# The third stage of a four-stage network on one Trainium2 core: routing first, experts behind 6.5 base tiles, and no arithmetic on GpSimd

## The chip, the core and the metric

The kernel runs on one core of a Trainium2 chip. The metric is the device time of one execution in microseconds (us), the median of several runs. The engines are TensorE (PE, matrix products), VectorE (DVE), ScalarE (ACT), GpSimd (POOL) and SyncE (SP, which here only issues DMAs); each has its own queue of instructions, and they wait for each other on semaphores.

## The reference

Four layers work one after the other on x of 2048 tokens by 1024 numbers (16 tiles of 128 tokens). Each is a mixing over 64 channels and then a feed-forward part, and is added to x. The change is in the third layer and in what it hands to the fourth:

```python
# third layer, feed-forward part (x: tokens y2, made by a convolution)
base_out = jnp.einsum('bsi,oi->bso', x, base_w) + base_b
res_hidden = jnp.einsum('bsi,ri->bsr', x, A)                 # 64 numbers a token
logits = jnp.einsum('bsi,ei->bse', x, router_w)              # 16 experts
topw, topi = jax.lax.top_k(jax.nn.softmax(logits, axis=-1), 2)
topw = topw / (jnp.sum(topw, axis=-1, keepdims=True) + 1e-06)
combine = jnp.sum(jax.nn.one_hot(topi, num_experts) * topw[..., None], axis=-2)
delta = jnp.einsum('bse,bsr,eor->bso', combine, res_hidden, B)
return base_out + delta * SCALING
# fourth layer: a 64x64 mixing matrix for each of the 32 sequences, then
return _layernorm(shared_out + routed_out, ln_gamma, ln_beta)
```

## The kernel before

Float32 products are made of two float32r parts, a high one that ScalarE rounds and a low one that VectorE subtracts; a product of two such pairs is three matmuls (hi·hi, hi·lo, lo·hi).

The third stage (`phase_l2`) has these parts. **Router**: `router` makes 80 columns a tile (16 logits, 64 numbers of `res`). `choose`, `weigh`, `rank` and `place_pairs` on VectorE, with `rank_pairs` on TensorE between them, find the two experts of every token and the place `pos` of its 4096 (token, expert) pairs in a list ordered by expert. GpSimd scatters the pairs there (32 indirect DMAs of 128 rows, to `scratch_pairs`). **Base**: for each of the 16 tiles `base_chunk(t, 0)` and `(t, 1)`, 24 matmuls of 128x512 each, into PSUM `po[t % 2]`; their input is y2 of the tile, loaded into one buffer (`l_y`), cut into `l_y2s_hi` and `l_y2s_lo`. `base_out` on VectorE adds the product to `x3[t]`, to which GpSimd (`base_bias`) has added the bias. **Experts**: 47 tiles of 128 pairs, in 12 groups of up to four. `turn_rows(g)` transposes the rows of a group (twice, a transpose for PSUM rows 0 to 63 and a product with the identity for rows 64 to 127), `r_high` and `r_low` cut them, `expert_tile(i)` makes four matmuls into one of three pairs of PSUM banks, ACT and DVE (`expert_out`) copy one half each into one of four buffers, and GpSimd writes the 128 rows to `scratch_expert_out` by an indirect DMA, whose row numbers lie in column 64 of the group's rows. `rows_in(g)` reads a group's rows into one of three buffers, once the expert rows of group g-3 are written. **Sum and mix**: per tile two rows of `delta` are read (`deltas_in`), GpSimd adds them (`delta_sum`), VectorE adds the sum to x3 (`add_deltas`), `mix(t)` makes 8 products of 128x128 on TensorE with the fourth layer's matrices, `y3_out` and `y3_low` (DVE) and a cut on ACT prepare the fourth layer's input, and GpSimd adds `beta` to x3, which SP stores for the fourth layer (`scratch_x3b`).

Every engine's order is written out by hand. Before, TensorE does base tiles 0 to 7 (the router of the last tiles and the ranking among them), then all experts, then eight blocks of one base tile and two mixes. The queue of SP holds all loads but those of B (4 DMAs of 2 MB, on ACT).

```python
def y2_in(t):
    sp.wait_ge(y2_lo, 2 * t)
    sp.dma_start(y2[:], tile_of(SC["y2T"], t))...
def rows_in(g):
    if g >= 3:
        sp.wait_ge(tr_mm, g - 2)
        for sem in eo_stored:
            sp.wait_ge(sem, 16 * (g - 2))
```

The fourth stage (`phase_l3`) is a long row of matmuls; at the end of each half of the tokens ACT loads x3b tile by tile and `finish(T)` on DVE adds it to the normalized tile.

## Time and profile before

| | |
|---|---|
| median of 3 runs | 1807.75 us (1804.79 to 1808.0) |
| the profiled execution | 1816.88 us, its span 1815.2 us |
| TensorE busy in the span | 1644.1 us (91%) |
| third stage, from the last convolutions to the gate of the fourth | 480.2 to 899.5 us |
| of it: up to the experts' first transpose | 480.2 to 604.4 us |
| of it: experts | 604.4 to 711.5 us |
| of it: eight blocks of a base tile and two mixes | 711.5 to 899.5 us |
| fourth stage's matmuls | 899.5 to 1797.6 us |

All times in the profile count from the span's start. "Busy" of TensorE includes the modelled end of each matmul: in an unbroken row a matmul of 128x512 is shown with 0.39 us, and the next starts 0.23 us after it.

### The profile page before, as it was taken

What the parts mean: (1) busy time and instruction counts of PE and PEld (TensorE: products, weight loads), DVE (VectorE), ACT (ScalarE), POOL (GpSimd) and SP (SyncE); (2) the same over time, 40 slices, a digit from 0 to 9 for tenths busy, and PEclk for the clock granted to TensorE, in tenths of its full rate; (3) what the DMA queues carried; (4) which work ended last, traced back from release to release, by engine and by line L of the source; (5) the groups of instructions that cost most, each with busy time, mean ns of one, the idle gap of its engine ahead of it and who ended that gap; (6) DMA issues with size and microseconds to landing.
All of it is one profiled execution on the core that took longest, in us unless ns stands there. A gap on an engine that the chain in (4) does not pass through costs nothing.

```text
span 1815.2 us, 20711 instructions
## 1 busy us (share of the span) xinstructions
PE 1644.1 (91%) x7830; PEld 1326.3 (73%) x7830; DVE 839.6 (46%) x1294; ACT 500.3 (28%) x763; POOL 423.2 (23%) x272
## 2 busy tenths in 40 slices
PE   6799678999897978776899999999999999999997
PEld 3688546988875646655678888888767888888875
DVE  5455458995274433654523333333282333333326
ACT  2344223333225332110032222221243222222112
POOL 1000111234245244555611111111251111111110
PEclk9999889999997988878999999999999999999999
DMA  8577444457831355455621111111462111111114
GB/s 280 132 176 168 152 77 151 161 179 234 312 141 53 115 214 197 165 187 202 232 91 47 47 47 46 46 46 47 134 214 70 47 47 47 46 46 46 47 58 162
DMA packets 108210, 222.82 MB, mean 123 GB/s; under 512 B 21892, under 2 KB 60924, under 8 KB 107260
## 3 DMA queue, kind: packets, MB, share of 16 engines
q1 hardware_dynamic: 86612, 161.00, 27.9%
q0 software_dynamic: 13120, 38.88, 6.6%
q10 hardware_dynamic: 8400, 21.89, 3.7%
q8 instruction: 51, 0.84, 0.2%
q14 instruction: 27, 0.22, 0.0%
HBM read 152.96 MB, written 76.61 MB: 126 GB/s over the span
## 4 chain that ended last, share of the span: by engine, by line
PE 67%; DMA 7%; DVE 4%; POOL 3%; issue 2%; ACT 2%; SPq 1%; another core or an unknown queue 1%; ACTq 0%; POOLq 0%; DVEq 0%
PE pd L1775 25%; PE pu L1775 24%; PE pf L1775 6%; PE l_po L1775 4%; DMA delta<-scratch_expert_out 3%; PE pw L390 2%; PE pw L391 2%; POOL l_x L1371 1%; PE l_ea L1213 1%; DMA scratch_expert_out<-expert_out,pair_rows 1%; PE l_po L1714 1%; DMA l_y<-scratch_y2T 1%; DMA pair_rows<-scratch_pairs 1%; PE pg L997 1%
## 5 line engine op out<-in xcount | busy, mean ns | idle before, releaser
L1910 POOL TENSOR_TENSOR down_lo<-raw,down_hi 128x1024 fp32r<-128x1024 f32 x40 | 100.3, 2508 | 698.2 <-ACT down_hi L1923 698.2
L1775 PE MATMUL pd<-down_hi,hid_hi 128*128 128x512 f32 x640 | 249.1, 389 | 2.9 <-issue 2.9
L1775 PE MATMUL pu<-y_hi,up_hi 128*128 128x512 f32 x640 | 249.2, 389 | 0.0
L1775 PE MATMUL pu<-y_hi,up_lo 128*128 128x512 f32 x640 | 249.0, 389 | 0.0
L1775 PE MATMUL pd<-down_hi,hid_lo 128*128 128x512 f32 x640 | 249.0, 389 | 0.0
L1775 PE MATMUL pd<-down_lo,hid_hi 128*128 128x512 f32 x640 | 249.0, 389 | 0.0
L1775 PE MATMUL pu<-y_lo,up_hi 128*128 128x512 f32 x640 | 249.0, 389 | 0.0
L2079 DVE TENSOR_TENSOR hid_lo<-hidden,hid_hi 128x512 fp32r<-128x512 f32 x64 | 44.3, 692 | 393.3 <-ACT hid_hi L1987 393.3
L2018 DVE TENSOR_TENSOR acc<-pd,acc 128x512 f32<-128x512 f32 x224 | 143.6, 686 | 54.7 <-PE pd L1775 51.4
L1981 ACT ACTIVATE hidden<-pu 128x512 f32<-128x512 f32 x64 | 38.3, 598 | 464.9 <-PE pu L1775 464.9
L1775 PEld LDWEIGHTS pd<-down_hi,hid_hi 128*128 128x128 f32 x640 | 120.2, 188 | 28.6 <-issue 3.7
L1775 PE MATMUL l_po<-l_base_hi,l_y2s_hi 128*128 128x512 f32 x256 | 108.3, 423 | 34.8 <-DVE l_y2s_lo L1463 32.9
L1775 PEld LDWEIGHTS pu<-y_hi,up_lo 128*128 128x128 f32 x640 | 120.2, 188 | 25.1
L1775 PEld LDWEIGHTS pu<-y_hi,up_hi 128*128 128x128 f32 x640 | 120.0, 188 | 25.1
L1775 PEld LDWEIGHTS pd<-down_hi,hid_lo 128*128 128x128 f32 x640 | 120.1, 188 | 25.1
L1775 PEld LDWEIGHTS pu<-y_lo,up_hi 128*128 128x128 f32 x640 | 120.2, 188 | 24.9
L1775 PEld LDWEIGHTS pd<-down_lo,hid_hi 128*128 128x128 f32 x640 | 120.1, 188 | 24.7
L1775 PE MATMUL pf<-cbT,z_hi 128*128 128x512 f32 x256 | 104.8, 409 | 5.0 <-DVE z_lo L880 5.0
L1775 PE MATMUL l_po<-l_base_lo,l_y2s_hi 128*128 128x512 f32 x256 | 106.4, 416 | 2.2 <-issue 2.2
L1775 PE MATMUL l_po<-l_base_hi,l_y2s_lo 128*128 128x512 f32 x256 | 105.5, 412 | 1.9 <-issue 1.9
L1775 PE MATMUL pf<-cbT,z_lo 128*128 128x512 f32 x256 | 101.8, 398 | 0.0
L1775 PEld LDWEIGHTS l_po<-l_base_hi,l_y2s_hi 128*128 128x128 f32 x256 | 52.2, 204 | 47.9 <-issue 36.0
(306 smaller groups left out, 2689.4 us busy)
## 6 DMA issues: line engine op xcount, KB each, us to landing
X<-scratch_x SPq DMA_DIRECT2D x256, 64.0 KB, 2.6
l_x<-scratch_x SPq DMA_DIRECT2D x32, 512.0 KB, 5.8
delta<-scratch_expert_out SPq DMA_DIRECT2D x32, 512.0 KB, 7.2
raw<-in_up SPq DMA_DIRECT2D x32, 512.0 KB, 3.7
raw<-in_down SPq DMA_DIRECT2D x32, 512.0 KB, 4.2
x_in<-in_x SPq DMA_DIRECT2D x16, 512.0 KB, 4.7
scratch_x<-x_in SPq DMA_DIRECT2D x16, 512.0 KB, 4.4
scratch_x<-l_x SPq DMA_DIRECT2D x16, 512.0 KB, 5.6
```

The source lines that it names most:

```text
L390: pe.matmul(cols, x[:, b * GROUPS + g, :], taps[0][:, g, :], start=True, stop=False)
L391: last = pe.matmul(cols, xs[:, b * GROUPS + g, :], taps[1][:, g, :], start=False, stop=True)
L997: last = pe.matmul(pg[n % 2][:], chunk[:, l, (k - at) * P:(k - at + 1) * P], K["exp"][:, l, :], start=l == 0, stop=l == NLAT - 1)
L1213: last = pe.matmul(ea[t % 2][:, 0:R2 + E2], prior["y2"][:, t % 2, k, :], war[:, k, :], start=k == 0, stop=k == KC - 1)
L1371: pool.tensor_tensor(x3[t][:], x3[t][:], beta[:], ALU.add).then_inc(x3b_made, 1)
L1714: last = pe.matmul(out_banks[i % 3][h][:], rT[g % 2][part][:, n * P:(n + 1) * P], B[:].rearrange("p e o -> p (e o)")[:, bass.ds(at + h * H ...
L1775: mm = pe.matmul(out, lhs[a], rhs[b], start=first and n == 0, stop=last and n == len(pairs) - 1)
L1910: pool.tensor_tensor(dn[u][i][1][:], raw[i][:], dn[u][i][0][:].bitcast(F32), ALU.subtract).then_inc(dn_lo, 1)
L1981: act.activation(act_f[:, k % 2, :], pu[q], ACT.Relu).then_inc(relu, 1)
L2018: last = dve.tensor_tensor(part, bank, part, ALU.add)
L2079: dve.tensor_tensor(hid[u][1][:, i, cols], pu[q] if lat else act_f[:, k % 2, :], hid[u][0][:, i, cols].bitcast(F32), ALU.subtract).then_in ...
```

## The change

- **Routing**: the last router products come before any further base work, and `choose` directly behind the last convolution's output.
- **Experts** start behind 6.5 base tiles (before: 8). The second half of base tile 6 is spread over the first eight groups, a few matmuls each; `po[0]` stays with it, so experts have two pairs of banks. The blocks behind are nine: the first has base tile 7 alone, the others a base tile and two mixes.
- **Rows**: ScalarE writes each row twice side by side (`pair_rows_twice`), and one transpose of 128 columns turns it. VectorE copies the row numbers out (`row_numbers`), so a buffer of rows is free without waiting for the stores.
- **y2** is loaded in halves, each when the same half of the tile before is cut. B comes in 8 DMAs of 1 MB on SP's queue, between them.
- **Bias** is a product of ones and two rows (high and low), two matmuls more per base tile.
- **GpSimd** computes nothing in this stage: VectorE adds both deltas itself, GpSimd's queue issues the stores of x3 and y3, ACT's queue the loads of the mixing matrices. `beta` is added in the fourth stage, by a DMA that adds to its destination.

```diff
-        def y2_in(t):
+        def y2_in(t, c):
             sp.wait_ge(prior["y2_stored"][t % 2], 16 * (t // 2 + 1))
-            sp.wait_ge(y2_lo, 2 * t)
-            sp.dma_start(y2[:], tile_of(SC["y2T"], t)).then_inc(y_loaded, 16)
+            sp.wait_ge(y2_lo, 2 * (t - 1) + c + 1)
+            sp.dma_start(y2[:, chunk(c)], tile_of(SC["y2T"], t)[:, chunk(c)]).then_inc(y_loaded[c], 16)
...
             if g >= 3:
-                sp.wait_ge(tr_mm, g - 2)
-                for sem in eo_stored:
-                    sp.wait_ge(sem, 16 * (g - 2))
+                sp.wait_ge(twice, g - 2)
+                sp.wait_ge(row_ids, g - 2)
...
-        delta_sum(0)
-        delta_sum(1)
...
+        for s in range(9):
+            for t in mixed_tiles(s):
+                pool.wait_ge(x3_made, t + 1)
+                pool.wait_ge(x3p_made, 2 * (t + 1))
+                pool.dma_start(tile_of(SC["x3b"], t), x3[t][:]).then_inc(x3b_stored[t % 4], 16)
...
         def add_deltas(t):
-            dve.wait_ge(d_sum, t + 1)
-            dve.wait_ge(x3p_made, 2 * (t + 1))
-            dve.tensor_tensor(x3[t][:], x3[t][:], d[t % 2][0][:], ALU.add).then_inc(x3_made, 1)
+            dve.wait_ge(d_loaded[t % 2], 32 * (t // 2 + 1))
...
+            dve.tensor_tensor(x3[t][:], x3[t][:], d[t % 2][0][:], ALU.add).then_inc(d_first, 1)
+            dve.wait_ge(d_first, t + 1)
+            dve.tensor_tensor(x3[t][:], x3[t][:], d[t % 2][1][:], ALU.add).then_inc(x3_made, 1)
...
-                pe.transpose(tr[g % 2][0:R2, cols], G[:, g % 3, n, 0:R2], K["ident"][:])
-                last = pe.matmul(tr[g % 2][R2:P, cols], G[:, g % 3, n, 0:R2], K["ident"][:], start=True, stop=True)
+                last = pe.transpose(tr[g % 2][:, n * P:(n + 1) * P], Gd[:, g % 2, n, :, :].rearrange("p u r -> p (u r)"), K["ident"][:])
...
-        router(pe, NT - 3)
-        base_chunk(0, 1)
         prior["conv"](pe, NT - 1)
         router(pe, NT - 2)
+        router(pe, NT - 1)
+        base_chunk(0, 1)
         base_chunk(1, 0)
-        router(pe, NT - 1)
+        rank_pairs()
         base_chunk(1, 1)
-        base_chunk(2, 0)
-        rank_pairs()
-        base_chunk(2, 1)
-        for t in range(3, 8):
+        for t in range(2, 6):
             base_chunk(t, 0)
             base_chunk(t, 1)
+        base_chunk(6, 0)
         turn_rows(0)
...
+            if g == 0:
+                base_start(6, 1)
+            if g < 8:
+                base_part(6, 4 + g // 2, g % 2)
+            if g == 8:
+                base_bias(6)
+        for s in range(9):
+            base_chunk(7 + s, 0)
+            base_chunk(7 + s, 1)
+            for t in mixed_tiles(s):
+                mix(t)
...
+        def add_beta(T):
+            pool.wait_ge(x3b_loaded[T % 2], 16 * (T // 2 + 1))
+            pool.dma_start(x3b[:, T % 2, :], A["L3_ffn_ln_beta"].partition_broadcast(P), accum_op=ALU.add).then_inc(beta_added[T % 2], 16)
...
-            dve.wait_ge(x3b_loaded[T % 2], 16 * (T // 2 + 1))
+            dve.wait_ge(beta_added[T % 2], 16 * (T // 2 + 1))
```

VectorE's queue around the last convolution (y2T) and the routing. Before:

```order
L705 TENSOR_TENSOR y2T<-pw,ctx 128x8x64 x2
L1463 TENSOR_TENSOR l_y2s_lo<-l_y,l_y2s_hi 128x512
L1469 TENSOR_TENSOR l_x_0<-l_po,l_x_0 128x512 x2
L1463 TENSOR_TENSOR l_y2s_lo<-l_y,l_y2s_hi 128x512
L1486 MEMSET route_taken 128x8
L1487 TENSOR_REDUCE route_m<-router_lg 128x16
```

And now:

```order
L1660 TENSOR_TENSOR l_bias<-l_bias_row,l_bias 1x1024
L1496 TENSOR_TENSOR l_y2s_lo<-l_y,l_y2s_hi 128x512
L706 TENSOR_TENSOR y2T<-pw,ctx 128x8x64 x2
L1519 MEMSET route_taken 128x8
L1520 TENSOR_REDUCE route_m<-router_lg 128x16
```

The two cuts of y2 and the first base tile's addition, which stood between the last convolution and the choice of experts, now stand behind the choice.

SP's queue in the blocks behind the experts, for two blocks. Before:

```order
L1237 DMA l_y<-scratch_y2T 128x1024
L1253 DMA delta<-scratch_expert_out 128x1024 x4
L1261 DMA mats<-scratch_mats 64x64 x2
L1262 DMA l_bias<-scratch_bias 128x128
L1266 DMA scratch_x3b<-l_x_2 128x1024
L1261 DMA mats<-scratch_mats 64x64 x2
L1262 DMA l_bias<-scratch_bias 128x128
L1266 DMA scratch_x3b<-l_x_3 128x1024
L1232 DMA l_x_11<-scratch_x 128x1024
L1232 DMA l_x_12<-scratch_x 128x1024
```

And now:

```order
L1258 DMA l_y<-scratch_y2T 128x512
L1275 DMA delta<-scratch_expert_out 128x1024 x4
L1258 DMA l_y<-scratch_y2T 128x512
L1246 DMA l_x_9<-scratch_x 128x1024
L1246 DMA l_x_10<-scratch_x 128x1024
L1258 DMA l_y<-scratch_y2T 128x512
L1275 DMA delta<-scratch_expert_out 128x1024 x4
```

The stores of x3 and the loads of the mixing matrices are no longer in this queue between two loads of deltas.

GpSimd's queue in the same place. Before:

```order
L1335 TENSOR_TENSOR delta<-delta 128x1024 x2
L1331 TENSOR_TENSOR l_x_9<-l_x_9,l_bias 128x1024
L1371 TENSOR_TENSOR l_x_2<-l_x_2,l_beta 128x1024
L1371 TENSOR_TENSOR l_x_3<-l_x_3,l_beta 128x1024
L1335 TENSOR_TENSOR delta<-delta 128x1024 x2
L1331 TENSOR_TENSOR l_x_10<-l_x_10,l_bias 128x1024
```

And now:

```order
L1383 DMA scratch_x3b<-l_x_8 128x1024
L1383 DMA scratch_x3b<-l_x_9 128x1024
L1387 DMA scratch_y<-l_y_0 128x1024
L1387 DMA scratch_y<-l_y_1 128x1024
L1383 DMA scratch_x3b<-l_x_10 128x1024
```

All additions have gone and two stores per block (four from tile 8 on) have come.

## Rows read from the trace of the kernel before

**Rows 1.** Stages: window, us, busy (count) PE PEld DVE ACT POOL, clock, DMA, GB/s

```profile
480.20:604.40 124.20, 103.78 (x458) 83.84 (x457) 62.76 (x104) 47.24 (x73) 53.22 (x43) 0.86 0.38 141
604.40:711.50 107.10, 89.13 (x347) 56.86 (x346) 42.08 (x63) 34.74 (x60) 45.93 (x47) 0.89 0.50 178
711.50:899.50 188.00, 136.33 (x625) 115.44 (x624) 96.85 (x85) 16.38 (x22) 105.12 (x39) 0.85 0.54 194
```

**Rows 2.** The chain that ended last: start us, us, what

```profile
487.49 4.73 issue
...
563.12 15.56 another core or an unknown queue
...
616.63 3.33 DMA scratch_expert_out<-expert_out,pair_rows
620.05 3.16 DMA pair_rows<-scratch_pairs
...
746.40 9.39 DMA delta<-scratch_expert_out
```

**Rows 3.** TensorE's timeline: start us, us, operation, count [idle before]

```profile
505.18 1.91 PE L1213 MATMUL l_ea<-l_war,y2T 128*128 128x80 f32 x16
...
521.71 0.41 PE L1687 MATMUL l_tr<-route_taken,ranks_below 128*128 128x272 bf16 x1 [3.68 <-DVE route_taken L1511]
...
604.44 0.27 PE L1700 MATMUL l_tr<-ident,pair_rows 128*64 128x128 f32 x1
604.64 0.43 PE L1701 MATMUL l_tr<-ident,pair_rows 128*64 128x128 f32 x2
...
742.32 2.05 PE L1725 MATMUL l_ea<-mats,l_x 128*128 128x128 f32 x16
```

**Rows 4.** Window of the base product alone, three tiles in a row

```profile
523.78:558.30 34.52, 34.49 (x144) 28.12 (x144) 2.56 (x4) 0.00 (x0) 0.95 0.20 61
```

**Rows 5.** GpSimd's timeline in the routing

```profile
513.70 4.92 POOL L1331 TENSOR_TENSOR l_x<-l_x,l_bias 128x1024 f32<-128x1024 f32 x2 [2.25 <-DMA l_x<-scratch_x]
```

**Rows 6.** VectorE's timeline in the routing

```profile
511.94 0.40 DVE L1487 TENSOR_REDUCE route_m<-router_lg 128x16 f32<-128x256 f32 x1
...
513.96 2.41 DVE L1496 TENSOR_TENSOR route_pick<-route_key,route_kmax 128x256 f32<-128x256 f32 x1
...
520.77 0.43 DVE L1509 TENSOR_TENSOR route_pick<-route_key,route_kmax 128x256 f32<-128x256 f32 x1
```

**Rows 7.** GpSimd's timeline: last pairs, first and last expert stores

```profile
532.54 1.07 POOL L1351 DMA_INDIRECT scratch_pairs<-pair_val,pair_pos  x1 [13.92 <-DVE pair_pos L1563]
...
574.67 0.96 POOL L1351 DMA_INDIRECT scratch_pairs<-pair_val,pair_pos  x1 [0.30 <-issue]
612.76 1.00 POOL L1357 DMA_INDIRECT scratch_expert_out<-expert_out,pair_rows  x1 [37.13 <-DVE expert_out L1585]
...
708.56 0.98 POOL L1357 DMA_INDIRECT scratch_expert_out<-expert_out,pair_rows  x1 [0.30 <-issue]
709.84 0.98 POOL L1357 DMA_INDIRECT scratch_expert_out<-expert_out,pair_rows  x1 [0.30 <-issue]
```

**Rows 8.** Waits behind the experts: us, times, longest

```profile
POOL delta L1335 <- DMA delta<-scratch_expert_out: 80.9, 11, 15.2
...
PE l_po L1775 <- DVE l_y2s_lo L1463: 25.8, 6, 6.1
```

**Rows 9.** The tile delta: ns min/median/max, and its DMA

```profile
L1590 DVE TENSOR_TENSOR l_x<-l_x,delta x16: 1211/3230/3420, 720.5 to 892.0; 128x1024 f32<-128x1024 f32 x16
...
DMA to landing us min/median/max: 3.4/7.2/9.4
```

**Rows 10.** The tile x3b of the fourth stage, from issue to landing

```profile
DMA to landing us min/median/max: 3.2/4.1/12.6
```

**Rows 11.** ACT at the end of the kernel

```profile
1800.73 0.33 ACTq L1926 DMA_DIRECT2D l_x3b<-scratch_x3b  x1
```

**Rows 12.** VectorE at the end of the kernel

```profile
1806.90 1.28 DVE L2038 SCALAR_TENSOR_TENSOR acc<-scratch,l_rstd,l_x3b 128x1024 f32<-128x1024 f32 x1
```

More of the change, by code:

```diff
@@ L1288, in sync @@
         sp.wait_ge(r_mm, NT)
+        sp.wait_ge(val_stored, 16 * 2 * NT)
+        for g in range(3):
+            rows_in(g)
+        sp.wait_ge(B_rest, E2)
         x3_in(6)
[L1290 to L1297 removed]
+        y2_in(7, 0)
+        for g in range(3, NGRP):
+            rows_in(g)
+            if g == 6:
+                y2_in(7, 1)
+        y2_in(8, 0)
+        sp.wait_ge(tr_mm, NGRP)
+        x3_in(7)
+        sp.wait_ge(twice, NGRP)
+        sp.wait_ge(row_ids, NGRP)
         x3_in(8)
@@ L1301, in sync @@
         deltas_in(1)
[L1302 to L1313 removed]
+        y2_in(8, 1)
@@ L1897, in body @@
             if end:
+                add_beta(HT * (half - 1))
+                add_beta(HT * (half - 1) + 1)
                 for t in range(HT):
```

492 lines of the change are left out of this document (267 added, 225 removed).

## The prediction

> **What bounds the kernel now.** I read the page's busy times first: TensorE is busy 91% of the span, so what can go is its idle time and its slow stretches. The windows by stage [rows 1] say where these are. The fourth stage has none to speak of (table above: one row of matmuls from 899.5 to 1797.6). The third stage takes 124.2 + 107.1 + 188.0 = 419.3 us, and in each of its parts the granted clock is 0.85 to 0.89, since the engine stops and starts. Then I read the chain that ended last [rows 2] for what stands between the matmuls. In the first part a wait of 4.73 us and one of 15.56 us stand out; TensorE also waits 3.68 us for the choice of experts [rows 3]. Among the experts a loop repeats every two groups: stores of expert rows (3.33 us), then the load of the next rows (3.16 us), then TensorE. Behind the experts the loop is: a load of deltas (9.39 us) that GpSimd waits for, and GpSimd's additions behind it. The waits of that part [rows 8] say the same: GpSimd waits 80.9 us for deltas and TensorE 25.8 us for the cut y2.
>
> **The change, part by part.** I use three measures. Base product: three tiles took 34.52 us [rows 4], 11.5 us each; without that window's small losses it is 48 matmuls by 0.227 us (the spacing in an unbroken row) = 10.9 us. Expert store: 709.84 - 708.56 = 1.28 us each on GpSimd [rows 7]. Mix: the 16 records of one tile take 2.05 us [rows 3], 1.95 without the start; two are 3.9 us.
>
> *First part (480.2 to 604.4).* Removed: 1.5 base tiles moved behind, 17.3 us; the wait of 4.73 us, because ScalarE no longer waits for y2 and 8 MB of B ahead of the last shifted tile; the wait of 3.68 us, because the choice starts right behind the last convolution and base products lie over it. It also gets shorter: VectorE's 128x256 operation takes 2.41 us while GpSimd adds and 0.43 us when it doesn't [rows 5, 6]. Removed, if it is what it looks like, the gap of 15.56 us. It lies inside the 43 us of GpSimd's 32 scatters, and no row names its cause; in the new order the scatters lie over base tiles too. I take it as gone, and price the other case as a rival. Added: two bias matmuls for 6 tiles, 12 by 0.23 = 2.7 us. Sum: 124.2 - 17.3 - 4.7 - 3.7 - 15.6 + 2.7 = 85.6 us, so the first transpose starts at 565.8. The scatter must be through by then. The last router product ended at 505.18 + 1.91 = 507.1 [rows 3]; without the wait of 4.7 us and with two base halves (10.9 us) behind it, it ends near 491.5. From the start of the choice to the first scatter it took 532.54 - 511.94 = 20.6 us [rows 6, 7], of which 4 us were the two stretched operations; so the scatter starts near 508.4. It takes 575.63 - 532.54 = 43.1 us [rows 7] and ends near 551.5; with 3.3 us for its stores and 3.16 us for the load [rows 2] the rows are there near 558. That is 8 us of cover.
>
> *Experts.* Since rows no longer wait for stores, GpSimd's 1.28 us a store should set the pace: 46 by 1.28 = 59 us between first and last. TensorE needs less for a group of four: 16 matmuls by 0.23 (3.7 us), four transposes by 0.20 (0.8 us, the spacing of L1700 and L1701 [rows 3]; before, three records a tile, 2.4 us), and 3 base matmuls (0.7 us), together 5.2 us against 5.13 us of GpSimd. Two PSUM pairs instead of three leave each pair about 1 us to be copied, which is near VectorE's time for it; so there is no slack here. First store 8.3 us after the first transpose before (612.76 - 604.44), less 2.7 us for the shorter transposes: 5.6 us. Last store 3.3 us to land. Sum 5.6 + 59 + 3.3 = 67.9 us, where it was 713.2 - 604.4 = 108.8 us.
>
> *Behind the experts.* TensorE leaves the experts 5.8 us before the last store has landed (four buffers and one copy ahead). Then a block of base tile 7, and eight blocks with a base tile and two mixes. A base tile with bias is 10.9 + 0.46 = 11.4 us; a block with mixes 11.4 + 3.9 = 15.3 us. The deltas must keep up: after the second pair of deltas is added, the next 2 MB are asked for, and the four loads take 7.2 to 9.4 us [rows 9]; VectorE's four additions take 1.21 us each where GpSimd is silent and 3.23 us in the median where it isn't [rows 9], so 4.9 us. With 0.7 us for the cut that SP waits for, this loop is 9.4 + 4.9 + 0.7 = 15.0 us, just under TensorE's 15.3. VectorE as a whole is busy 96.85/8 = 12.1 us a block now [rows 1], and 16 additions more are paid by shorter ones. I take 16 us a block, a little above both. Sum: 2 by 11.4 - 5.8 + 3.9 + 7 by 16 = 132.9 us to the gate, where it was 899.5 - 713.2 = 186.3 us.
>
> *Halves of y2.* The half of the next tile is asked for one whole tile ahead, and the 25.8 us of waits [rows 8] are in the 53 us that this part gives; nothing is counted twice. *B on SP's queue*: 1 MB ahead of a half of y2 is two loads of 512 KB, of which the second of a pair landed in 7.2 us in the median [rows 9], against a cover of 11.4 - 1.5 us for the cut; nothing, though the slowest (9.4 us) would come close. *Stores on GpSimd's queue and matrices on ACT's*: both engines are idle most of this part (16.38 us of 188 busy on ACT [rows 1]); nothing.
>
> *Beta in the fourth stage.* The trace has no adding DMA. The nearest row is the load of the same tile, 3.2 to 12.6 us, 4.1 in the median [rows 10]; below nothing it can't be. In a tile's rhythm of 5.4 us, a load and an addition have two rhythms, 9.6 us, so 4.1 + 4.1 is hidden. At the very end it isn't: the last load is issued at 1800.73 [rows 11] and used at 1806.90 [rows 12], 6.2 us for 3.2 + 0.5 + 4.1 = 7.8 us. I take 2 us there and 2 us at the end of the first half: +4 us (0 to 18). By the Trainium skill (DMA: Bandwidth & Descriptors, anatomy of the GpSimd path) such a DMA costs 2.0 us plus its bytes at 436 GB/s, an estimate of 3.2 us; by that the end would cost 1 us less. No run here shows it yet.
>
> *Total.* First part 124.2 - 85.6 = 38.6, experts 40.9, behind 53.4, less 4: 128.9 us. From the profiled execution's 1816.9 us that is 1688 us. The median of the runs is 9.1 us lower (1807.75), which would give 1679. But if the gap of 15.6 us is only in profiled executions, the runs give 1807.75 - 113.3 = 1694. I take the middle: **1686 us**, own range 1665 to 1702.
>
> **The rivals.**
> - *Deltas hold the blocks.* 4.5 MB a block in 15.3 us is 294 GB/s, where the part ran at 194 [rows 1]; if loads queue longer (14 us for four), a block takes 20 us: 8 by 4 = +32, **1718 us**. For it: every row of delta's chain is at its limit. Against: the DMA share was 0.54.
> - *The gap stays.* Whatever stops the engines inside the scatter does so again: +16, **1702 us**. For it: it lies in the scatter. Against: the scatter starts 30 us before it [rows 2, 7], and TensorE ran through most of these [rows 4].
> - *Experts slower than GpSimd's pace.* Two PSUM pairs, and more work on ACT and DVE: 1.6 us a tile, +15, **1701 us**.
> - *GpSimd's stores are held by VectorE.* Each store waits out an addition, x3's next tile comes late, and a block takes 18 us: +16, **1702 us**. Against it: GpSimd's indirect DMAs took 0.96 to 1.07 us all along [rows 7], while VectorE worked beside them. [...]
> - *Slower than before.* The adding DMA, with 128 rows read from the same 4 KB, could take so long that it sets the rhythm of the fourth stage's 16 last tiles. To eat 129 us, each must lose 8 us: (4.1 + y)/2 = 13.5, so y = 23 us. Above that the kernel is slower than before; at 30 us, 1686 + 16 by 3.5 + 129, about **1870 us**. The worst load of the tile took 12.6 us, which speaks against it.
> - *It does nothing*, because one queue (SP) still couples all loops: its largest waits were for stores of experts, which are gone. **1808 us**.
>
> **How the numbers follow.** Forecast 0.50; deltas 0.20; gap 0.10; experts 0.10; stores held 0.05; slower 0.03; nothing 0.02. The range must hold the first five, of which the slowest reaches some way beyond 1718, and below the forecast the case that all pieces reach TensorE's pace (1686 less 6 for the blocks, 6 for the first part and 9 for the median's lead over the profile): 1665 to 1735. What a measurement of this kernel can tell from no change is 0.2%, 3.6 us. Faster 0.95, same 0.02, slower 0.03.
>
> **What would show it.** Right: no idle time of TensorE over 3 us between 486 and the experts; expert stores 1.28 us apart without the pauses of 5.5 us; starts of base tiles 15.3 to 16 us apart behind them; granted clock near 1 in all three; VectorE's additions at 1.2 us. Wrong: base tiles 20 us apart with TensorE waiting for x3 (deltas); a pause of 15 us inside the scatter; stores 1.6 us apart and TensorE waiting for copies; x3 loads late behind stores; VectorE waiting for beta in each of the 16 last tiles. If TensorE waits for rows at its first transpose, the 8 us of cover were wrong.

## The result, and the profile after

The changed kernel takes **1733.9 us** in the median of 4 runs (1733.3 to 1743.1), the kernel before on the same chip 1807.9 (1804.8 to 1810.2): ratio 0.960, 95% interval 0.956 to 0.963. It is faster, by 74 us; the forecast was 1686 us and a range of 1665 to 1735 us, and 122 us of gain. The profiled execution of the changed kernel took 1743.05 us, 55 us more than the 1688 us that the sum gave for it. (On two other chips the kernel before took 1822 to 1842 us and the changed one 1732 to 1748 us, ratios 0.950 and 0.949.)

The windows of the changed kernel by stage; the columns are those of [rows 1]. The first window ends where the base product of the third stage begins, then come the part up to the first turned rows, the experts, the part behind them, and the fourth stage with the end.

```profile
core 0: us, PE busy (x) PEld busy (x) DVE busy (x) ACT busy (x) POOL busy (x), PEclk, DMA share, GB/s
0.00:483.70 483.70, 418.82 (x2397) 339.18 (x2397) 296.82 (x516) 162.13 (x258) 79.42 (x71) 0.93 0.60 166
483.70:573.60 89.90, 89.90 (x455) 73.39 (x455) 54.11 (x88) 46.23 (x59) 39.21 (x36) 1.00 0.65 210
573.60:658.00 84.40, 66.27 (x263) 44.31 (x262) 42.50 (x73) 39.97 (x71) 44.32 (x46) 0.96 0.66 237
658.00:792.25 134.25, 134.25 (x706) 111.35 (x705) 88.17 (x106) 19.48 (x26) 14.19 (x25) 1.00 0.78 284
792.25:1741.30 949.05, 900.83 (x3955) 732.22 (x3953) 348.45 (x526) 238.85 (x348) 150.23 (x90) 0.98 0.25 77
```

In the first part and behind the experts TensorE now has no idle time at all and a granted clock of 1.00; of the stages that the prediction priced, only the experts and the fourth have any idle time. Set beside the forecast, piece by piece:

| piece, us | before | forecast | measured |
|---|---|---|---|
| start to base product | 471.0 | 471.0 | 483.7 |
| to the first turned rows | 133.5 | 94.9 | 89.9 |
| experts, until TensorE leaves them | 102.5 | 62.1 | 84.3 |
| behind them, to the gate | 192.6 | 138.7 | 134.3 |
| fourth stage to the end | 915.7 | 919.7 | 949.1 |

(Forecast: the prediction's sums with its own borders moved; 62.1 is 67.9 - 5.8.) The miss of 55 us is 12.7 ahead of the base product, in stages that the change hardly touches, 22.2 at the experts and 29.4 in the fourth stage, less 5.0 and 4.4 us where it went better than forecast.

The fourth stage does its upward and downward products in two halves, each closed by a part of eight tiles that are normalized ("first end", before the second gate; "second end", before the end of the kernel). Windows of the changed kernel:

```profile
792.25:1197.56 405.31, 403.86 (x1788) 329.16 (x1786) 135.86 (x201) 103.25 (x146) 53.02 (x25) 1.00 0.17 56
1197.56:1263.56 66.00, 46.99 (x192) 37.67 (x192) 41.79 (x61) 18.63 (x29) 32.78 (x28) 0.88 0.93 252
1263.56:1670.89 407.33, 405.88 (x1784) 329.54 (x1785) 136.79 (x201) 104.67 (x149) 53.03 (x22) 0.99 0.15 51
1670.89:1741.30 70.41, 44.09 (x192) 35.85 (x192) 34.01 (x64) 12.30 (x24) 11.40 (x16) 0.84 0.68 178
```

Both long stretches are as before. The two ends take 66.0 and 70.4 us; from the same starting points (first downward product, at 1304.79 and 1759.15) they took 47.6 and 56.0 before. That is where the 33 us are. What happens to one buffer there is read from three timelines of the changed kernel, in this order ScalarE's queue (load of x3), GpSimd (adding DMA) and VectorE (the use):

```profile
1222.34 0.33 ACTq L2003 DMA_DIRECT2D l_x3b<-scratch_x3b  x1
1235.72 0.33 ACTq L2003 DMA_DIRECT2D l_x3b<-scratch_x3b  x1
```

```profile
1205.27 0.93 POOL L1966 DMA_DIRECT2D l_x3b<-in_L_ffn_ln_beta  x1 [2.47 <-DMA l_x3b<-scratch_x3b]
1226.50 0.86 POOL L1966 DMA_DIRECT2D l_x3b<-in_L_ffn_ln_beta  x1 [3.32 <-DMA l_x3b<-scratch_x3b]
```

```profile
1221.02 1.28 DVE L2115 SCALAR_TENSOR_TENSOR acc<-scratch,l_rstd,l_x3b 128x1024 f32<-128x1024 f32 x1 [10.44 <-DMA l_x3b<-in_L_ffn_ln_beta]
1233.58 2.11 DVE L2115 SCALAR_TENSOR_TENSOR acc<-scratch,l_rstd,l_x3b 128x1024 f32<-128x1024 f32 x1 [1.06 <-DMA l_x3b<-in_L_ffn_ln_beta]
```

The load is asked for at 1222.34 and has landed by 1226.50, when beta is asked for; that has landed by 1233.58, VectorE uses the buffer for 2.1 us, and its next load goes out at 1235.72: 13.4 us for one round, with two buffers and a rhythm of 5.44 us a tile. In the mean of the six rounds of each end a round took 13.3 and 13.7 us: the load 4.1 and 4.7, GpSimd's issue 0.3 behind its landing, the adding DMA 6.8 and 7.1, and VectorE's wait and use 2.1 and 1.5. The very first addition of beta, asked for at 1205.27, had landed by 1221.02, behind 4 MB of y in the same queue. The list of DMA issues has the medians from issue to landing (last column):

```profile
l_x3b<-scratch_x3b ACTq DMA_DIRECT2D x16, 512.0 KB, 4.1
l_x3b<-in_L_ffn_ln_beta POOLq DMA_DIRECT2D x16, 512.0 KB, 6.8
```

At the first end TensorE then waits for VectorE to take its products out of PSUM into `acc`, 19.0 of 19.5 us in all, 12.0 of them ahead of the second gate:

```profile
PE pd L1845 <- DVE acc L2091: 19.5, 4, 12.0
```

```profile
1245.82 0.50 PE L1845 MATMUL pd<-down_hi,hid_hi 128*128 128x512 f32 x1 [1.51 <-DVE acc L2091]
1263.56 0.59 PE L1845 MATMUL pd<-y_hi,gate_hi 128*8 128x512 f32 x1 [12.01 <-DVE acc L2091]
```

At the second end it is not TensorE that waits. Its 192 products take 44.6 us (43.8 before), and the time is lost behind them: 25.8 us to the end of the kernel, where it was 12.2. The last of VectorE's waits for beta lie there:

```profile
1670.89:1715.49 44.60, 44.09 (x192) 35.85 (x192) 25.79 (x52) 10.37 (x20) 8.62 (x12) 1.00 0.74 190
1715.49:1741.30 25.81, 0.01 (x1) 0.00 (x0) 8.21 (x12) 1.93 (x5) 2.78 (x5) 0.56 0.58 158
```

```profile
1718.24 1.28 DVE L2115 SCALAR_TENSOR_TENSOR acc<-scratch,l_rstd,l_x3b 128x1024 f32<-128x1024 f32 x1 [3.86 <-DMA l_x3b<-in_L_ffn_ln_beta]
1724.49 1.28 DVE L2115 SCALAR_TENSOR_TENSOR acc<-scratch,l_rstd,l_x3b 128x1024 f32<-128x1024 f32 x1 [3.51 <-DMA l_x3b<-in_L_ffn_ln_beta]
```

At the experts, the waits of TensorE in the changed kernel between 573 and 660 us (us in all, times, longest), and four of GpSimd's stores:

```profile
PE l_ea L1778 <- DVE expert_out L1623: 6.3, 5, 1.6
PE l_ea L1778 <- ACT expert_out L1423: 4.4, 4, 2.5
PE l_po L1778 <- issue: 3.1, 7, 1.0
```

```profile
600.55 0.98 POOL L1377 DMA_INDIRECT scratch_expert_out<-expert_out,pair_ids  x1 [0.30 <-issue]
602.63 0.97 POOL L1377 DMA_INDIRECT scratch_expert_out<-expert_out,pair_ids  x1 [1.10 <-ACT expert_out L1423]
603.91 0.98 POOL L1377 DMA_INDIRECT scratch_expert_out<-expert_out,pair_ids  x1 [0.30 <-issue]
606.39 0.97 POOL L1377 DMA_INDIRECT scratch_expert_out<-expert_out,pair_ids  x1 [1.50 <-DVE pair_ids L1612]
```

Of the pauses of 6.5 to 9.7 us before, one of 5.25 us near the end is left, but stores now come in twos, 1.3 to 1.7 and then 1.5 to 3.0 us apart: 47 stores from 579.36 to 659.52, 1.74 us each, where the forecast had 1.28.

### The profile page after: what moved, and what is told of

Read it like the earlier page. It is cut to its first block, busy times and chain, and to the rows that moved or that the text cites. A ratio compares the mean times of both kernels' runs of the same rounds, so it can differ in the third digit from the quotient of the medians.

```text
span 1741.3 us, 20651 instructions
## 1 busy us (share of the span) xinstructions
PE 1610.1 (92%) x7768; PEld 1300.5 (75%) x7768; DVE 830.0 (48%) x1307; ACT 506.7 (29%) x761; POOL 327.4 (19%) x266
## 4 chain that ended last, share of the span: by engine, by line
PE 74%; DMA 7%; DVE 3%; issue 1%; ACT 1%; POOL 0%; ACTq 0%; DVEq 0%; POOLq 0%
PE pu L1845 25%; PE pd L1845 22%; PE l_po L1845 10%; PE pf L1845 6%; DMA l_x3b<-in_L_ffn_ln_beta 3%; DMA l_x3b<-scratch_x3b 2%; PE pw L392 2%; PE pw L391 2%; PE l_ea L1221 2%; PE l_ea L1778 1%; DMA scratch_expert_out<-expert_out,pair_ids 1%; DMA scratch_g<-latent_out 1%; PE l_po L1778 1%; PE pg L998 1%; PE l_ea L1793 1%
## 5 line engine op out<-in xcount | busy, mean ns | idle before, releaser
L1845 PE MATMUL pd<-down_hi,hid_hi 128*128 128x512 f32 x640 | 250.7, 392 | 10.4 <-DVE acc L2091 7.5
L1845 PE MATMUL l_po<-l_base_hi,l_y2s_hi 128*128 128x512 f32 x256 | 101.3, 396 | 0.0
L1845 PE MATMUL l_po<-l_base_hi,l_y2s_lo 128*128 128x512 f32 x256 | 99.8, 390 | 0.0
L1845 PE MATMUL l_po<-l_base_lo,l_y2s_hi 128*128 128x512 f32 x256 | 99.8, 390 | 0.0
L405 ACT COPY Xs<-X 64x1016 f32<-64x1016 f32 x32 | 33.3, 1042 | 139.0 <-DMA X<-scratch_x 139.0
```

Source lines behind the costliest of these rows:

```text
L405: act.copy(xs[0:CH, :, 0:P - 1], x[0:CH, :, 1:P]).then_inc(sem, 1)
L1845: mm = pe.matmul(out, lhs[a], rhs[b], start=first and n == 0, stop=last and n == len(pairs) - 1)
```

## The experiments

Pieces are measured as above, in each kernel's profiled execution: "fourth stage" from the gate to the end, "experts" from the first turned rows until TensorE leaves them, "behind" from there to the gate. Totals are medians; "the changed kernel" is 1733.9 us on the first chip, 1738.0 and 1738.9 us on two others.

**What beta costs.** Beta left out:

```python
-                    if t + 2 < HT:
-                        add_beta(T + 2)
-            dve.wait_ge(beta_added[T % 2], 16 * (T // 2 + 1))
+            dve.wait_ge(x3b_loaded[T % 2], 16 * (T // 2 + 1))
```

Expected: 

> The changed kernel, and beta is left out of the output: no adding DMA, the rest as it is. In the changed kernel the fourth stage takes 949.0 us from its gate to the end, before 915.7, 33 us more. Theory A (the adding DMA, behind a load in a ring of two buffers, makes 13.3 us for two tiles where the matmuls want 10.9, and the last one lies bare): the fourth stage falls back to 915 to 917 us, total about 1701 us. Theory B (an adding DMA costs what the nearest load does, 4 us, and the stage is longer for another reason, such as gamma's load or the place of the third stage's last stores): at most 5 us of the 33 come back, total about 1729 us. The first two stages took 471 us before and 484 us in the changed kernel: if that goes by the placement of tiles it is 484 here again; if by chance, it may be anything between.

Measured: 1707.5 us, ratio 0.944 (0.942 to 0.947); fourth stage 917.3 us. Its windows for the two ends:

```profile
1193.50:1241.10 47.60, 43.76 (x192) 35.93 (x193) 36.24 (x61) 18.66 (x29) 28.20 (x20) 0.99 0.83 262
1647.54:1705.50 57.96, 43.80 (x192) 35.94 (x192) 34.26 (x64) 12.29 (x24) 4.30 (x8) 0.90 0.44 144
```

The ends take 47.6 and 58.0 us and the fourth stage is within a microsecond of theory A; the total is 6.5 us above it. The other way round, the kernel before with the same adding DMA put in:

```python
+        def add_beta(T):
+            pool.wait_ge(x3b_loaded[T % 2], 16 * (T // 2 + 1))
+            pool.dma_start(x3b[:, T % 2, :], A["L3_ffn_ln_beta"].partition_broadcast(P), accum_op=ALU.add)...
```

Expected: 

> The kernel before, and besides its own addition of beta the fourth stage gets the changed kernel's adding DMA (so beta is in the output twice); the third stage is untouched. Theory A: its fourth stage goes from 915.7 to 946 to 949 us, total 1808 + 31 = 1839 us. Theory B: at most 5 us more, 1813 us. The first two stages: 471 us if the placement of tiles decides.

Measured: 1841.5 us, ratio 1.017 (1.013 to 1.020); fourth stage 951.5 us, its ends 66.4 and 71.5 us. Theory A again. (In the medians beta costs 26 us by the first of these two runs, 1733.9 less 1707.5, and 32 us by the second, 1841.5 less the 1809.8 of the kernel before beside it; the 33 us are those of the profiled execution.) The profile has something more, which counts below: the third stage here is that of the kernel before, and its part ahead of the first turned rows took

```profile
487.46:602.51 115.05, 106.42 (x515) 89.87 (x515) 63.76 (x105) 49.24 (x77) 55.11 (x43) 0.94 0.50 183
```

18.4 us less than the 133.5 us before. Of the kernel before, the stretch of its timeline that stood as a gap of 15.56 us in [rows 2]:

```profile
558.28:580.25 21.97, 9.96 (x25) 5.57 (x25) 5.19 (x9) 5.82 (x9) 13.38 (x14) 0.65 0.16 45
```

TensorE did 25 matmuls in 22 us there, single ones with 0.2 to 1.2 us of "issue" ahead of them, and then waited 6.4 us for a cut of y2. In the other execution, with the same third stage, 264 base matmuls stood in an unbroken row from 540.77 to 602.68. **The kernel can run without the gap**: of two executions one had it. What made it is not shown.

**Where else beta could be added.** In DRAM, in the third stage:

```python
+        def beta_in_dram(t):
+            pool.wait_ge(x3b_stored[t % 4], 16 * (t // 4 + 1))
+            pool.dma_start(tile_of(SC["x3b"], t), A["L3_ffn_ln_beta"].partition_broadcast(P), accum_op=ALU.add)...
```

Expected: 

> The changed kernel, with the adding DMA of each tile moved from the fourth into the third stage: it adds beta to the stored rows in DRAM, two tiles behind, where nothing waits for it. Theory A: fourth stage 915 to 917 us; the third stage stays at 15.35 us a block since TensorE bounds it; total 1701 us, as without beta. Rival C: the 16 adding DMAs (read and write 512 KB each in DRAM) take DMA time from deltas and x3 in a part whose DMA share is already 0.6 to 0.97: blocks of 17 us and more, total 1715 us or above. Theory B: total 1730 us.

Measured: 1738.9 us, ratio 0.962 (0.959 to 0.965). The fourth stage is 918.7 us, but the part behind the experts 168.2 us instead of 134.3: blocks of 15.4, 16.4, 20.5, 19.9, 21.3, 21.9 and 26.0 us. Its list of DMA issues says why, rival C:

```profile
delta<-scratch_expert_out SPq DMA_DIRECT2D x32, 512.0 KB, 10.3
scratch_x3b<-in_L_ffn_ln_beta POOLq DMA_DIRECT2D x16, 512.0 KB, 12.9
```

The adding DMAs take 12.9 us, and the deltas 10.3 instead of 6.3. The 34 us have only moved.

**Why it costs that much.** Two kernels on the ring. The first asks for the first two additions ahead of y's loads:

```python
-            if end and front:
-                load_y(g)
             if end:
                 add_beta(HT * (half - 1))
                 add_beta(HT * (half - 1) + 1)
+                if front:
+                    load_y(g)
```

Expected: 

> The changed kernel, with one thing moved: at the end of the first half GpSimd asks for the adding DMAs of the half's first two tiles ahead of the eight loads of y instead of behind them. In the changed kernel the first of them, asked for at 1205.3, was behind 4 MB of y on the same queue and VectorE waited 10.4 us for it. If its place in the queue matters (theory A1), the first half's end gets 7 to 10 us shorter (66.0 us from its first product to the gate now), total 1725 to 1727 us; if the ring of two buffers alone sets it (theory A2), that end stays within 3 us of 66 and the total at 1731 to 1734 us.

Measured: 1735.0 us, first end 67.2 us: nothing gained (A2), though the first additions now landed within 9 us instead of 15.6. The second has three buffers and the same order:

```python
-                if 0 < T % HT < HT - 1:
-                    load(T + 1)
+                if 0 < T % HT < HT - 2:
+                    load(T + 2)
```

Expected: 

> The changed kernel, with a third buffer for x3 + beta in the fourth stage (in the place of the relu values, which are not in use there), so load and adding DMA have three tiles' time instead of two, and the adding DMAs of the first three tiles ahead of y's loads. Theory A2 (a load of about 4 us, an adding DMA of about 7 us from issue to landing and VectorE's 1.3 us are one chain per buffer: 13.3 us, for two buffers more than 2 by 5.44 us, for three less than 16.3): both ends fall back nearly to those of before, the fourth stage to 917 to 922 us, total 1702 to 1708 us, as with beta left out. Rival (the adding DMAs and loads hold each other's bandwidth or the queue, so a third buffer only makes them longer): less than 12 us of the 33 come back, 1722 us or more.

Measured: 1724.0 us, fourth stage 939.2 us: the second end fell from 70.4 to 61.6 us, the first only to 64.8, where ScalarE waited 13.4 us for y. 10 of 33 us came back, as the rival had it (less than 12, 1722 us or more), and its reason shows too: with three buffers the load took 5.9 us in the median instead of 4.1 and the adding DMA 7.4 instead of 6.8. The ring of two was most of the cost at the second end, and at the first it was not. Then the adding itself, made a plain DMA (x3 is left out of the output):

```python
-            ....partition_broadcast(P), accum_op=ALU.add).then_inc(beta_added[T % 2], 16)
+            ....partition_broadcast(P)).then_inc(beta_added[T % 2], 16)
```

Expected: 

> The changed kernel, whose adding DMA is made a plain one of the same shape, same queue and same waits: beta then overwrites x3, which is left out of the output. Theory K (it is the adding that takes long: 6.8 us in the median from issue to landing, the plain load of x3 beside it about 4): the plain DMA lands in about 4 us, and the fourth stage falls from 949 to 925 us or less, total 1710 us. Theory L (what costs is a second DMA in the chain behind the first, with GpSimd's issue and the stores before it in the same queue, adding or not): fourth stage 940 to 949 us, total 1725 to 1735 us.

Measured: 1730.3 us, fourth stage 941.4 us, 63.0 and 66.3 us at the ends. From issue to landing the plain one took 5.0 us in the median where the adding one took 6.8. So adding as such is 8 of the 33 us (theory L); the changed kernel on the same chip took 1738.0 us and 949.6 in this stage. Y's loads on another queue, with three buffers:

```python
-                    pool.dma_start(y_raw[:, :, cols:cols + P], ...
+                    act.dma_start(y_raw[:, :, cols:cols + P], ...
```

Expected: 

> The kernel with three buffers for x3 + beta, and y's eight loads at the end of the first half go to ScalarE's queue, so that on GpSimd's only the adding DMAs and the output's stores are left. The third buffer alone gave back 10 us of the 33: 9 at the second end and 1 at the first, where ScalarE then waited 13.4 us for y's loads behind the adding DMAs. Theory M (the two kinds of transfers in one queue hold each other there): the first end falls from 64.8 us to 50 us, fourth stage 939 - 14 = 925 us, total 1710 us. Theory N (it is the sum of the DMAs' time, not the queue): first end 60 us or more, fourth stage 935 us or more, total 1720 us or more.

Measured: 1737.9 us, fourth stage 947.9, first end 71.1 us, worse than before the move. The numbers are within theory N's, but ScalarE's timeline shows a cost that neither theory had; the eight loads held its queue for 24 us (with three loads of x3 and three additions under way), and the normalization stood behind them:

```profile
1196.06 24.18 ACTq L1995 DMA_DIRECT2D y_raw<-scratch_y  x8
1220.34 1.12 ACT L2017 ACTIVATE pu<-acc,l_neg_mean 128x1024 f32<-128x1024 f32 x1 [25.65 <-issue]
```

**One adding DMA a tile.** ScalarE copies beta into the buffer, and the DMA that brings x3 adds it on top:

```python
-            act.dma_start(x3b[:, T % 2, :], tile_of(SC["x3b"], T)).then_inc(x3b_loaded[T % 2], 16)
+            act.copy(x3b[:, T % 2, :], act_f[:]...).then_inc(filled, 1)
-            pool.dma_start(x3b[:, T % 2, :], A["L3_ffn_ln_beta"].partition_broadcast(P), accum_op=ALU.add)...
+            pool.wait_ge(filled, T + 1)
+            pool.dma_start(x3b[:, T % 2, :], tile_of(SC["x3b"], T), accum_op=ALU.add)...
```

Expected: 

> The changed kernel with two buffers, in which the order of the sum is turned: beta is loaded once per half, ScalarE copies it into the buffer (about 1.05 us), and one adding DMA brings the tile of x3 from DRAM onto it, so each tile has one DMA in its chain instead of two; y's loads are on ScalarE's queue. The chain is 1.05 + 6.8 + 1.3 = 9.2 us for a buffer, under 10.9. Theory A2: fourth stage 918 to 924 us, total 1703 to 1710 us. Rival (an adding DMA cannot come every 5.44 us at all): VectorE waits for beta at most tiles of both ends, fourth stage 935 us or more.

Measured: 1724.6 us, ratio 0.943; ends 60.5 and 61.8 us, fourth stage 935.5. At the second end the additions kept the rhythm of 5.44 us without a wait until the last two tiles; at the first ScalarE's issue of y's loads took 14.6 us. So the total missed theory A2 by 15 us, and the rival's sign, waits at most tiles of both ends, is not there either. Then with y's loads back on GpSimd's queue and the first two buffers filled ahead of them:

```python
+            if lat and u == 1:
+                act.dma_start(act_f[:]..., A["L3_ffn_ln_beta"].partition_broadcast(P)).then_inc(x3b_loaded[0], 16)
+                act.wait_ge(x3b_loaded[0], 16 * (half + 1))
+                load(HT * half)
+                load(HT * half + 1)
```

Expected: 

> The changed kernel, with the turned sum (ScalarE copies beta into the buffer, one adding DMA brings the tile of x3), beta loaded and the first two tiles' buffers filled and added one group of products before each end, and y's loads where the changed kernel has them. With the turned sum alone the adding DMAs kept a rhythm of 5.44 us at the second end without a wait, and only the last one lay bare; the first end lost its 13 us at the start, where ScalarE was held 14.6 us by the issue of y's loads. If the place in the chain is what costs, and not the adding: first end 48 to 52 us (66 to 68 in the changed kernel, 47.6 in the one before), second end 58 to 61 us (70 and 56.0), fourth stage 920 to 926 us, total 25 us under the changed kernel on the same chip. If the adding itself costs, both ends stay above 60 us.

Measured: **1719.7 us, ratio 0.939 (0.936 to 0.943)**, fourth stage 930.4. VectorE's timeline at the second end:

```profile
1679.76 1.28 DVE L2122 SCALAR_TENSOR_TENSOR acc<-scratch,l_rstd,l_x3b 128x1024 f32<-128x1024 f32 x1
1685.20 1.28 DVE L2122 SCALAR_TENSOR_TENSOR acc<-scratch,l_rstd,l_x3b 128x1024 f32<-128x1024 f32 x1
1690.64 1.29 DVE L2122 SCALAR_TENSOR_TENSOR acc<-scratch,l_rstd,l_x3b 128x1024 f32<-128x1024 f32 x1
```

That is 19 us under the changed kernel beside it, where 25 were expected. VectorE's use comes every 5.44 us without a wait; this end is 58.8 us, against 58.0 without beta. The first is 59.2 us, not the 48 to 52 expected: ScalarE reached the copies only when the end had begun (1199.26), y's loads went out behind the additions at 1202.54, and it waited for y:

```profile
1216.25 1.05 ACT L2020 CAST y_hi<-y_raw 128x1024 fp32r<-128x1024 f32 x1 [10.77 <-DMA y_raw<-scratch_y]
```

The changed kernel unaltered, beside the last four runs told here, on their two chips:

Expected: 

> The changed kernel once more, unaltered, as the measure on this chip. In fourteen profiled executions so far the base product of the third stage began between 471.0 and 487.5 us, whatever kernel it was; the kernel before had the lowest of these, the changed kernel the third highest. If that start is chance it is again somewhere in 471 to 487; if the changed kernel's placement sets it, it is 484. Third stage from base to gate 308 to 311 us, fourth stage 949 us either way.

Expected: 

> The changed kernel, unaltered, a third time, as the measure for the kernel beside it on the same chip: third stage 308 to 310 us from base to gate, fourth stage 949 us; base product beginning anywhere from 471 to 487 us.

Measured: 1738.0 and 1738.9 us, fourth stage 949.6 and 951.2, base product from 479.7 and 484.1. Over all twenty profiled executions it began between 471.0 and 487.5 us; the two with the third stage of the kernel before had the lowest and the highest. So nothing ties the 12.7 us to the change.

**The experts.** Three pairs of PSUM banks, the base tile between them moved behind:

```python
-    out_banks = [ea, po[1]]
+    out_banks = [ea, po[0], po[1]]
```

Expected: 

> The changed kernel, with three pairs of PSUM banks for the experts' products instead of two; the half base tile that lay between them, and the other half ahead of them, go behind the experts. Theory D (two pairs hold the pace: 1.71 us a tile, TensorE waits for the copies out of the pair): stores come every 1.35 us or less, the 47 tiles take 64 us instead of 80.2 us between first and last store; the moved product keeps its 11 us, of which 5.5 lay inside the experts: total about 1734 - 17 + 5 = 1722 us. Theory E (the stores on GpSimd's queue and their landing in four buffers hold the pace): the pace stays at 1.65 us or above and the total rises to about 1738 us.

Measured: 1743.9 us, ratio 0.965. Neither theory held as a whole: stores came every 1.53 us instead of 1.74, but the experts are 75.5 us where 84.3 less the moved product (5.9) is 78.4. Now ScalarE waits for one of the four row buffers to be stored:

```profile
ACT expert_out L1423 <- DMA scratch_expert_out<-expert_out,pair_ids: 27.0, 31, 4.0
```

And the first turned rows came 4.2 us late, since 5.5 us of cover were gone: the forecast's 8 us of cover were 1.3. Base tile 6 whole ahead of the experts, with three pairs:

Expected: 

> The changed kernel, with base tile 6 whole ahead of the experts (its second half lay between them) and three pairs of PSUM banks for the experts. With three pairs and half tiles moved behind, stores came every 1.53 us instead of 1.74, and the copies waited 48 us in all for one of the four row buffers to be stored: there the rows were 4.2 us late for the first transpose, which this order covers. Theory: first part 89.9 + 5.9 = 95.8 us without a wait, experts 84.3 - 5.9 - 3 to 6 = 73 to 76 us, behind them 134.3 us; total 3 to 6 us under the changed kernel, 1728 to 1731 us. Rival (the pace is set by the copies' own work on ScalarE and VectorE): experts 78.4 us, total 1734 us.

Measured: 1740.8 us; stores every 1.59 us, experts 77.6, nearer to the rival's 78.4 than to 73 to 76. And a fifth row buffer with it:

Expected: 

> As the kernel with base tile 6 ahead and three pairs, and a fifth buffer for expert rows, in y2's place. Theory (a buffer's round is copy 0.7, issue 1.0 to 1.3 and landing about 4, together 6.1 us, so four buffers allow a store each 1.53 us and five one each 1.22 us, less than GpSimd's 1.28): stores come every 1.28 to 1.38 us, experts 62 to 66 us, total 1718 to 1722 us. Rival (landing takes longer the closer the stores come, or the next rows are late): stores at 1.45 us or slower, total above 1726 us. In either case y2's tile 8 is asked for only behind the last store, which costs nothing if it is cut within 11.4 us.

Measured: 1735.8 us, experts 79.4, where theory had 62 to 66. The copies' waits for stored rows fell from 37.5 us in the kernel just above to 7.6, stores came 1.28 us apart, but for one pause of 3.7 to 4.0 us at nearly every eighth, as in this row:

```profile
606.65 0.97 POOL L1376 DMA_INDIRECT scratch_expert_out<-expert_out,pair_ids  x1 [2.74 <-ACT expert_out L1422]
```

So the pace was 1.74, 1.53 to 1.59 and, pauses counted, 1.63 us a store: limits within 15% of each other, PSUM pairs, row buffers and the link behind the last pause, and taking one or two away shows the next. Which link makes that pause was not tried. The loads of rows made to wait for stores again:

```python
+                for sem in eo_stored:
+                    sp.wait_ge(sem, 16 * (g - 2))
```

Expected: 

> The changed kernel, with one part undone: the loads of expert rows wait again for the stores of the group three before, as in the kernel before, where that loop (stores 3.3 us, load 3.2 us, turned and cut) made pauses of 6.5 to 9.7 us in GpSimd's stores once every two groups. The buffers of rows are three and now freed early. Theory I (the wait for stores was the pause): pauses come back, experts 84.3 + 15 = 99 us or more, total 1750 us. Rival J (the three buffers give enough lead even so, and what made the pauses before was that y2, B and x3 stood in the same queue): experts within 3 us of 84.3, total 1734 to 1737 us.

Measured: 1766.5 us, ratio 0.969; experts 108.9 us. Theory I: pauses between stores are back, 4.3 to 7.0 us once a group, while ScalarE waits for the rows:

```profile
ACT pair_twice L1412 <- DMA pair_rows<-scratch_pairs: 44.9, 9, 6.8
```

This part of the change is worth 24.6 us.

**The blocks.** GpSimd adds the deltas again:

```python
+            pool.tensor_tensor(d[t % 2][0][:], d[t % 2][0][:], d[t % 2][1][:], ALU.add).then_inc(d_first, 1)
```

Expected: 

> The changed kernel, with one part undone: GpSimd adds the two deltas of a tile, as before, and VectorE only their sum to x3 (one addition a tile instead of two). Theory F (GpSimd's arithmetic was what held the blocks: VectorE's work beside it takes two to three times as long, and the deltas' buffers come free late): blocks of 18 us and more instead of 15.35, total 1734 + 20 = 1755 us. Rival G (halves of y2 and stores off the one queue gave the gain, GpSimd's arithmetic was harmless): blocks stay at 15.4 to 16 us, total 1734 to 1739 us.

Measured: 1751.2 us, ratio 0.960 (0.957 to 0.964); behind the experts 149.8 us, blocks of 15.4 to 20.1. The time is as theory F had it, the cause only in part: VectorE's addition took 1.35 us in the mean, hardly more than alone, but GpSimd's takes 2.67 us, and both stand in the loop of the deltas' buffers:

```profile
L1381 POOL TENSOR_TENSOR delta<-delta 128x1024 f32<-128x1024 f32 x16 | 42.7, 2669 | 91.5 <-DMA delta<-scratch_expert_out 91.5
L1638 DVE TENSOR_TENSOR l_x<-l_x,delta 128x1024 f32<-128x1024 f32 x16 | 21.4, 1353 | 42.9 <-POOL delta L1381 42.9
```

Y2 asked for as whole tiles again:

```python
-            sp.wait_ge(y2_lo, 2 * (t - 1) + c + 1)
+            sp.wait_ge(y2_lo, 2 * t if t >= 8 else 2 * (t - 1) + c + 1)
```

Expected: 

> The changed kernel, with one part undone in the part behind the experts: both halves of the next y2 tile are asked for only when both halves of the one before are cut, as with whole tiles. Then half 0 can be loaded only while half 1 of the tile before is multiplied (5.5 us), and takes 4 to 6 us and 1.3 us for the cut. If the halves matter (theory H, by the 25.8 us of TensorE's waits for the cut before), blocks take 16.5 to 18 us instead of 15.35 and the total is 1743 to 1755 us; if not, total within 3 us of 1734 us.

Measured: 1734.5 us; behind the experts 141.0 us instead of 134.3, in the last three blocks. In the total it can't be told from the changed kernel. Halves gave 7 us at most, and not as theory H had it: TensorE waits there ahead of the mixes, for x3 with its deltas and for nothing shown, and never for a cut of y2.

```profile
PE l_tr L1793 <- issue: 3.2, 1, 3.2
PE l_tr L1793 <- DVE l_x L1633: 2.3, 2, 1.6
```

**All together**, three pairs, five row buffers and three x3 + beta buffers:

Expected: 

> The changed kernel with all that the runs spoke for: base tile 6 ahead, three pairs and five buffers for the experts, and three buffers for x3 + beta with the first adding DMAs ahead of y's loads. If the two gains add: third stage 12 to 16 us and fourth stage 27 to 31 us shorter than the changed kernel, total 1734 - 41 = 1690 to 1695 us.

Measured: 1729.4 us, ratio 0.949, 34 to 39 us above what was expected. The experts' part gave nothing (309.5 us from base to gate, 308.5 in the changed kernel) and the ring 9 us. The best version is the one with the buffers filled early: on one chip 1719.7 us, where the changed kernel takes 1738.9 and the one before 1829.0.

## Why the prediction was wrong

The direction and most of the mechanisms held; the size failed: the median lies 48 us above the forecast, 32 us above its own narrower range (1665 to 1702), at the very end of the wide one.

- **The step that failed is the term for beta in the fourth stage, "+4 us (0 to 18)".** It measured +33 in the profiled execution, +30 to 36 in ten others with the same ring, and +2 without beta. The sentence "a load and an addition have two rhythms, 9.6 us, so 4.1 + 4.1 is hidden" had the right loop and the wrong price for the adding DMA. The nearest row, a load of the same tile at 4.1 us, was not near enough: on that queue a plain DMA took 5.0 and an adding one 6.8 us, so load, issue and addition were 11.2 and 12.2 us at the two ends instead of 8.2, and a round 13.3 and 13.7 where 10.9 are there.
- **The same term, what else it left out.** By an estimate from these rounds, six refills an end and 1.2 to 1.4 us lost at each make 7 to 9 us of the 18.4 and 14.4 us by which the ends grew. The rest was not in the prediction either. At the first end the two first additions meet 4 MB of y; VectorE waits 10.4 us for them, and asking for them first only moved the wait to y (ScalarE then waits 10.9 us). Behind TensorE's last product the loop lies bare for more than the one tile that the prediction priced. The upper bound, 18, had no sum behind it. The slower rival had the right place and the right mechanism, with a break-even at y = 23 us; at y = 6.8 its own formula, (4.1 + y)/2, gives 5.45 us a tile and no loss, while the kernel lost a quarter of the forecast gain.
- The estimate of 3.2 us that the prediction worked out from the Trainium skill (DMA: Bandwidth & Descriptors, anatomy of the GpSimd path) is not borne out for the adding DMA: the trace has 5.0 us at the least and 6.8 in the median, so the measurement decides against it for this kind.
- **Experts: wrong in size.** "GpSimd's 1.28 us a store should set the pace" measured 1.74; the term was 62.1 and is 84.3 us. The rival had 1.6 us and +15; its reason, two PSUM pairs and copies, is one of the three limits above. That rows don't wait for stores was right: 24.6 us.
- **First part: right in total by an error.** From base to turned rows 89.9 us against 94.9. But 15.6 of the forecast gain was a gap of one execution. Against the 115.1 us of the other execution the part gained 25 us, not 44. The prediction saw this chance, gave half of it to the median and 0.10 to a rival; the gap didn't come again in any profile. Whether it was in runs that were not profiled is not shown; the sum without it, below, fits their median. Of the 8 us of cover 1.3 were left: the first transpose came 5.0 us sooner behind the base product's start than forecast, and the last scatter 84.1 us behind it where the prediction's numbers make 80.5.
- **Behind the experts: right.** Blocks of 15.35 us (forecast 15.3 to 16), no wait for deltas, y2 or stores. Additions are back at 1.22 us. The rivals on deltas and on GpSimd's stores held by VectorE didn't come: expert stores took 0.97 us in the median as before (1.37 at the most), and the stores of x3 between VectorE's additions 0.53 to 0.61. The 7.2 us that the prediction gave to the second load of a pair is the median of all loads of deltas; its term was nothing and stayed so.
- **Stages ahead of the change: not in the sum.** 12.7 us between two executions, within the 16 us by which all twenty vary.

Set against the execution without the gap, the 74 us are about 25 in the first part (115.1 to 89.9), 17 at the experts (101.5 to 84.3) and 61 behind them (195.7 to 134.3, the old values from the kernel before with the adding DMA), less 33: 70 us, and a rest of 4 in the stages that vary.

**What stays open.** Of beta's 33 us, 8 are the adding (plain DMA), and the second end is cleared by one DMA a tile. At the first end at least 12 us remain with every order tried on two queues; y's loads on SP's queue were not tried. What makes the base product's start vary by 16 us is not shown either.

## What to carry to other kernels

Work moved out of a crowded stage into an "idle" one is priced by the whole round of the buffer it lands in: landing, issue, what stands ahead in that queue, and use, against buffers times rhythm. Here a round was a quarter too long, and every tile paid. A price taken from the nearest row needs a margin when the kind of transfer is another. A gap that no row names, in one profiled execution, is worth a second profile before it enters a sum; so is the length of stages that the change doesn't touch. Where several limits lie within 15% of the pace, as at the experts here, removing one gives almost nothing.

## What the runs showed of the hardware

- An adding DMA of 512 KB into SBUF took 6.8 us in the median from issue to landing, a plain one in its place 5.0, a load from ScalarE's queue beside it 4.1; into DRAM an adding one took 12.9 us, and the loads of deltas beside it 10.3 instead of 6.3. Where the adding DMA brought x3's tile instead of beta's one row for all partitions, it took 5.7 and 5.8 us, in kernels with fewer transfers beside it.
- Eight DMAs of 512 KB issued by ScalarE in a row held it for 14.6 and 24.2 us; from GpSimd the same eight took 7.1 us to issue.
- TensorE's clock has a part in the first end. After the wait of 5.49 us its granted clock was 0.50 and its matmuls stood 0.43 us apart instead of 0.23, the lower of its two levels (1.2 and 2.4 GHz), until 1230.4, so a wait cost more than its length; behind the wait of 12.01 us the first 4.6 us of the next part ran so too. At the second end it has none: the clock was 1.00 until TensorE's last product, and the 0.84 of that window is the time behind it.

```profile
1225.09 0.79 PE L1845 MATMUL pd<-down_hi,hid_hi 128*128 128x512 f32 x1 [5.49 <-DVE acc L2091]
1225.68 0.63 PE L1845 MATMUL pd<-down_lo,hid_hi 128*128 128x512 f32 x1
1226.11 0.63 PE L1845 MATMUL pd<-down_hi,hid_lo 128*128 128x512 f32 x1
```

- The kernel before took 1808 us in the median in the first comparison, 1810 on the chip of the first experiments and 1822 to 1829 us on four others, 0.8 to 1.2% more; the changed kernel, on two of these four, 0.2 to 0.3% more. So a ratio moved from 0.960 to 0.949 with the chip, and the kernels here are compared piece by piece in their profiles.
